# A message stage of a graph network: groups of four tiles, thin products padded to 128 rows, and a wait ahead of each pair of gathers

## What is computed

```
yv = edge_sh[:, 1:4]
m_s_tp = einsum('emi,ei->em', vs, yv) / sqrt(3)
w = silu(radial @ W_r1 * 8**-0.5) @ W_r2 * 8**-0.5
w_ss, w_vs, w_vt, w_st = split(w, 4, axis=1)
m_s = concat([ss * w_ss, m_s_tp * w_st])
m_v = concat([vs * w_vs, (ss x yv) * w_vt])
S, V = segment_sum(m_s, receivers), segment_sum(m_v, receivers)
```

## Time and profile before

| | us |
|---|---|
| median of 3 runs | 18873.3 |
| lowest, highest | 18834.3, 18887.8 |
| profiled execution | 18882.2 |
| its span | 18880.5 |

### The profile page before, as it was taken

The page is one execution under the profiler, slowest core; times in us unless marked ns, Lnnn a source line. Parts: engine busy times, 40 slices in busy tenths (PEclk is TensorE's granted clock), DMA queues, the critical chain, the costliest instruction groups (busy, mean ns, idle before and its releaser), DMA issues. The chain is left out here.

```text
span 18880.5 us, 358760 instructions
## 1 busy us (share of the span) xinstructions
PE 12828.6 (68%) x67608; PEld 9891.8 (52%) x67609; DVE 10946.8 (58%) x52171; ACT 4449.2 (24%) x12149; POOL 10487.9 (56%) x15826
## 2 busy tenths in 40 slices
PE   4457666666555556874888888759999998533333
PEld 2246666665333334763777777536666666422223
DVE  7778888886333334874565655426777775333333
ACT  7742222222111111441333333221111111200001
POOL 8878888887555554221555555205555552366664
PEclk9998999997555555996999999875555555655555
DMA  3001111111221112761555555401111112111113
GB/s 139 0 14 29 32 30 32 30 32 36 58 57 57 57 56 80 217 184 62 156 155 154 155 154 154 93 11 39 39 39 39 39 39 28 48 43 43 42 43 48
DMA packets 1925627, 1302.37 MB, mean 69 GB/s; under 512 B 1295244, under 2 KB 1680251, under 8 KB 1925564
## 3 DMA queue, kind: packets, MB, share of 16 engines
q1 hardware_dynamic: 1601276, 599.63, 14.0%
q0 software_dynamic: 324288, 701.98, 13.7%
HBM read 933.67 MB, written 373.78 MB: 69 GB/s over the span
## 5 line engine op out<-in xcount | busy, mean ns | idle before, releaser
L951 POOL DMA_INDIRECT edge_sv<-tab,edge_ix x1664 | 1569.0, 943 | 2169.5 <-DVE edge_ix L1332 1745.0
L951 POOL DMA_INDIRECT edge_fs<-tab_a,edge_ix x1664 | 1572.8, 945 | 1631.1 <-DVE edge_ix L1044 1176.4
L1759 POOL DMA_INDIRECT edge_ys<-tab,edge_ix x1664 | 1577.5, 948 | 1353.1 <-ACT edge_dl L1750 788.9
L610 POOL DMA_INDIRECT by_src<-send_row,send_pl x1664 | 1615.2, 971 | 1257.7 <-issue 1089.6
L662 PE MATMUL send_psX<-x_res,send_ohT 128*128 x3328 | 1315.1, 499 | 1188.9 <-ACT send_ohT L643 1077.5
L1803 PE MATMUL edge_psA<-edge_ys,edge_oh 128*128 128x128 f32 x3328 | 861.3, 441 | 1713.9 <-DVE edge_oh L1783 664.4
L460 POOL DMA_INDIRECT records<-place_pl,place_place x1568 | 1615.7, 1030 | 530.3 <-issue 492.1
L977 DVE TENSOR_TENSOR agg<-agg,edge_psA 128x256 f32 x3328 | 1379.7, 415 | 718.3 <-issue 358.0
L662 PEld LDWEIGHTS send_psX<-x_res,send_ohT 128*128 128x128 f32 x3328 | 833.5, 311 | 1758.9 <-issue 1758.9
L1803 PEld LDWEIGHTS edge_psA<-edge_ys,edge_oh 128*128 128x128 f32 x3328 | 740.9, 328 | 1834.4 <-DVE agg L1792 1355.5
L1398 PE MATMUL edge_psA<-edge_oh,edge_m 128*128 128x128 f32 x6656 | 1593.3, 421 | 0.6 <-DVE edge_m L1367 0.6
(11 more groups left out here) (319 smaller groups left out, 31986.0 us busy)
## 6 DMA issues: line engine op xcount, KB each, us to landing
edge_fd<-tab_b SPq DMA_DIRECT2D x1664, 128.0 KB
max_row<-by_src SPq DMA_DIRECT2D x392, 258.0 KB
running<-max_back POOLq DMA_DIRECT2D x392, 256.0 KB
records<-count_tmpl SPq DMA_DIRECT2D x64, 858.0 KB
send_pl<-records SPq DMA_DIRECT2D x832, 66.0 KB
edge_pl<-records SPq DMA_DIRECT2D x832, 50.0 KB
place_pl<-in_edge_attr SPq DMA_DIRECT2D x781, 50.0 KB
by_src<-send_row,send_pl POOLq DMA_INDIRECT x1664
```

Of the source, the lines that this page charges most:

```text
L610: pool.indirect_dma_start(S.by_src[:], bass.IndirectOffsetOnAxis(ap=at, axis=0), row[b][:, k, :], None, bounds_check=bound, oob_is_err=Fal ...
L951: pool.indirect_dma_start(rows[b % len(rows)][:, k, :], None, table[:], bass.IndirectOffsetOnAxis(ap=ix[b][:, k:k + 1], axis=0)).then_inc( ...
L1759: pool.indirect_dma_start(ys[b][:, k, :], None, table, bass.IndirectOffsetOnAxis(ap=ix[b][:, k:k + 1], axis=0)).then_inc(s_got[b], 16)
```

## The change

- Groups of four tiles (416 of them). Each group has one load, one transpose, one radial product, one weights product over 512 columns, and VectorE's message operations work on four tiles at once. `psA` takes two banks a group; `psT` and `psR` have one bank each instead of two.
- The radial and the weights product go over all 128 rows of their operands. The rows beyond 48 and 32 are zero; GpSimd clears them at the start.
- The one-hot moves from VectorE to ScalarE: four times Abs(dl - iota), then Relu(1 - gap) over 512 columns. ScalarE also copies indices and receiver rows (`ix`, `dl`). `sv`, `ix` and `dl` have four buffers, so the copy waits for the messages and the one-hot of the group four before.
- Block numbers are read four at once. The adds, and the message operations, stand in turns in VectorE's order.
- GpSimd waits, ahead of each pair of gathers, until the pair before the last one has landed (`paced`).

Lines that only rename G2 to G, and lines taken away whose counterpart is shown, are left out.

```diff
+def paced(pool, s_got, s_turn, b, r, depth, back):
+    o, n = before(b, r, back, depth)
+    if not isinstance(n, int) or n > 0:
+        pool.wait_ge(s_got[o], n * 32)
+        pool.sem_inc(s_turn, 1)
 def edge2_phase(nc, S, a, agg):
     with Phase(nc, "edge2") as ph:
-        M = 32
-        DEEP = 8
+        M, G, DEEP, NSV = 32, 4, 8, 4
...
+        ix = ph.sbs("ix", NSV, [P, G], I32)
+        dl = ph.sbs("dl", NSV, [P, G])
+        sv = ph.sbs("sv", NSV, [P, G, D])
...
+        oh = ph.sbs("oh", 2, [P, G, P])
         rT = ph.sbs("rT", 2, [P, P])
         hr = ph.sbs("hr", 2, [P, P])
-        vy = ph.sbs("vy", 2, [P, G2, 3, M])
...
-        psT = [ph.bank(f"psT{k}") for k in range(2)]
-        psR = [ph.bank(f"psR{k}") for k in range(2)]
...
+        m = ph.sbs("m", 2, [P, G, 2 * D])
+        wr1 = ph.sb("wr1", [P, G * 8])
+        wr2 = ph.sb("wr2", [P, G, D])
+        psT, psR = ph.bank("psT"), ph.bank("psR")
         psW = [ph.bank(f"psW{k}") for k in range(2)]
...
+        psA = [[ph.bank(f"psA{k}{h}") for h in range(2)] for k in range(2)]
...
+        s_got = [ph.sems(n, DEEP) for n in ("s_got_a", "s_got_b")]
...
         @block.sync
         def _(sp):
...
+            for k in range(G):
...
             def step(s, g, b, r):
                 wait(sp, s_m[b], r)
...
+                sp.dma_start(at[b][:], rec[:, bass.ds(g * G, G), R0:R0 + RN]).then_inc(s_rec[b], 16)
             runs(GT, [0], DEEP, sp, step)
         @block.gpsimd
         def _(pool):
...
-                 lambda s, g, b, r: gather_on(pool, b, ix, sv, S.tab_2, s_ix, s_got, s_turn, r))
+            for t in (wr1, wr2, *rT, *hr):
+                pool.memset(t[:], 0.0).then_inc(s_pad, 1)
+            pool.memset(one[:], 1.0).then_inc(s_pad, 1)
+            def step(s, g, b, r):
+                pool.wait_ge(s_ix[b], r + 1)
+                pool.sem_inc(s_turn, 1)
+                for k in range(G):
+                    if k % 2 == 0:
+                        paced(pool, s_got[k // 2], s_turn, b, r, DEEP, 1)
+                    pool.indirect_dma_start(sv[b % NSV][:, k, :], None, S.tab_2[:],
+                                            bass.IndirectOffsetOnAxis(ap=ix[b % NSV][:, k:k + 1], axis=0)
+                                            ).then_inc(s_got[k // 2][b], 16)
+            runs(GT, [0], DEEP, pool, step)
+        @block.scalar
+        def _(act):
+            act.wait_ge(s_pad, 7)
+            def step(s, g, b, r):
+                if s == 0:
+                    o, n = before(b, r, NSV, DEEP)
+                    wait(act, s_m[o], n)
+                    wait(act, s_oh[o], n)
+                    act.activation(ix[b % NSV][:], S.e_src[:, bass.ds(g * G, G)], ACT.Copy)
+                    act.activation(dl[b % NSV][:], S.e_dl[:, bass.ds(g * G, G)], ACT.Copy).then_inc(s_ix[b], 1)
+                elif s == 1:
+                    act.wait_ge(s_R[b], r + 1)
+                    o, n = two_before(b, r, DEEP)
+                    wait(act, s_W[o], n)
+                    act.activation(hr[b % 2][0:8 * G, :], psR[0:8 * G, 0:P], ACT.Silu, scale=8 ** -0.5).then_inc(s_hr[b], 1)
+                elif s == 2:
+                    act.wait_ge(s_T[b], r + 1)
+                    o, n = two_before(b, r, DEEP)
+                    wait(act, s_R[o], n)
+                    act.activation(rT[b % 2][0:G * RN, :], psT[0:G * RN, 0:P], ACT.Copy).then_inc(s_TT[b], 1)
+                else:
+                    act.wait_ge(s_ix[b], r + 1)
+                    o, n = before(b, r, 1, DEEP)
+                    wait(act, s_oh[o], n)
+                    for k in range(G):
+                        act.activation(gap[:, k, :], S.iota[:], ACT.Abs, scale=-1.0, bias=dl[b % NSV][:, k:k + 1]
+                                       ).then_inc(s_gap, 1)
+                    o, n = two_before(b, r, DEEP)
+                    wait(act, s_C[o], n)
+                    act.wait_ge(s_gap, g * G + G)
+                    act.activation(oh[b % 2][:], gap[:], ACT.Relu, scale=-1.0, bias=one[:]).then_inc(s_oh[b], 1)
+            runs(GT, [0, 1, 0, 2], DEEP, act, step)
         @block.vector
         def _(v):
...
+            v.memset(agg[:], 0.0).then_inc(s_add, 1)
...
+            def add(g, b, r, k):
+                half = psA[b % 2][k // 2]
+                rows = agg[:, bass.ds(blocks[k], 1), :].rearrange("p a c -> p (a c)")
+                if k == 0:
+                    v.wait_ge(s_C[b], r + 1)
+                v.wait_ge(s_add, g * G + k + 1)
+                v.tensor_tensor(rows, rows, half[:, (k % 2) * 2 * D:(k % 2 + 1) * 2 * D], ALU.add).then_inc(s_add, 1)
...
+            def step(s, g, b, r):
                 if s == 0:
...
+                    blocks[:] = nc.values_load_multi_w_load_instructions(
+                        S.blk[0:1, bass.ds(g * G, G)], engines=[mybir.EngineType.DVE], min_val=0, max_val=NBLK - 1)[1]
+                    return
+                if s in (2, 4, 6, 9):
+                    add(g, b, r, (2, 4, 6, 9).index(s))
+                    return
...
+                if s == 1:
+                    v.wait_ge(s_rec[b], (r + 1) * 16)
+                    v.wait_ge(s_got[0][b], (r + 1) * 32)
+                    v.wait_ge(s_got[1][b], (r + 1) * 32)
+                    o, n = two_before(b, r, DEEP)
+                    wait(v, s_C[o], n)
+                    v.tensor_tensor(vo[:, :, :, M:], vs, yv, ALU.mult).then_inc(s_op, 1)
+                elif s == 3:
+                    v.wait_ge(s_W[b], r + 1)
+                    v.tensor_tensor(su[b % 2][:], w[:, :, 2 * M:3 * M], ss, ALU.mult).then_inc(s_op, 1)
+                elif s == 5:
+                    v.wait_ge(s_op, g * OPS + 1)
+                    v.tensor_reduce(dot[b % 2][:], vo[:, :, :, M:].rearrange("p k i m -> p k m i"), axis=AX.X,
+                                    op=ALU.add).then_inc(s_op, 1)
                 elif s == 7:
...
-                    one_hot(v, oh[p][:], S, S.e_dl, g).then_inc(s_oh[b], 1)
...
+                    v.tensor_tensor(mo[:, :, 0:M], w[:, :, 0:M], ss, ALU.mult)
+                elif s == 8:
+                    v.tensor_tensor(vo[:, :, :, 0:M], thrice(w[:, :, M:2 * M]), vs, ALU.mult)
+                elif s == 10:
+                    v.wait_ge(s_op, g * OPS + 3)
+                    v.tensor_tensor(vo[:, :, :, M:], thrice(su[b % 2][:]), yv, ALU.mult).then_inc(s_op, 1)
                 else:
...
-            runs(GT, [0, 6, 4, 6, 4, 6, 4, 4], DEEP, v, lambda s, *x: step((0, 7, 1, 2, 3, 4, 5, 6)[s], *x))
...
-            runs(GT, [1, 2], DEEP, act, step)
+                    v.tensor_tensor(mo[:, :, M:2 * M], w[:, :, 3 * M:], dot[b % 2][:], ALU.mult).then_inc(s_m[b], 1)
+            runs(GT, [2, 0, 2, 0, 2, 0, 2, 0, 0, 2, 0, 0], DEEP, v, step)
         @block.tensor
         def _(pe):
...
+            pe.wait_ge(s_zero, 2)
+            pe.wait_ge(s_pad, 6)
             def step(s, g, b, r):
                 o, n = two_before(b, r, DEEP)
+                p, q = before(b, r, 1, DEEP)
                 if s == 0:
                     pe.wait_ge(s_m[b], r + 1)
                     pe.wait_ge(s_oh[b], r + 1)
...
+                    if not isinstance(g, int) or g >= 2:
+                        pe.wait_ge(s_add, (g - 2) * G + G + 1)
+                    for k in range(G):
...
+                            c = (k % 2) * 2 * D + q * D
+                            last = pe.matmul(psA[b % 2][k // 2][:, c:c + D], m[b % 2][:, k, q * D:(q + 1) * D],
                                              oh[b % 2][:, k, :], start=True, stop=True)
                     last.then_inc(s_C[b], 1)
                 elif s == 1:
                     pe.wait_ge(s_hr[b], r + 1)
                     wait(pe, s_m[o], n)
-                    pe.matmul(psW[b % 2][:, 0:G2 * D], hr[b % 2][0:8 * G2, :], wr2[0:8 * G2].rearrange("p k c -> p (k c)"),
+                    pe.matmul(psW[b % 2][:, :], hr[b % 2][:], wr2[:].rearrange("p k c -> p (k c)"),
                               start=True, stop=True).then_inc(s_W[b], 1)
                 elif s == 2:
                     pe.wait_ge(s_TT[b], r + 1)
...
-                    pe.matmul(psR[b % 2][0:8 * G2, 0:P], wr1[0:G2 * RN].rearrange("p k c -> p (k c)"), rT[b % 2][0:G2 * RN, :], start=True,
-                              stop=True).then_inc(s_R[b], 1)
+                    wait(pe, s_hr[p], q)
+                    pe.matmul(psR[0:8 * G, 0:P], wr1[:], rT[b % 2][:], start=True, stop=True).then_inc(s_R[b], 1)
                 else:
                     pe.wait_ge(s_rec[b], (r + 1) * 16)
...
-            runs(GT, [5, 3, 2, 1], DEEP, pe, step)
+                    wait(pe, s_TT[p], q)
+                    pe.sem_inc(s_go, 1)
+                    pe.transpose(psT[0:G * RN, 0:P], at[b][:].rearrange("p k c -> p (k c)"), S.ident[:]).then_inc(s_T[b], 1)
+            runs(GT, [4, 2, 1, 0], DEEP, pe, step)
```

More of the change, by code:

```diff
@@ L1274, in edge2_phase @@
-        sv = ph.sbs("sv", DEEP, [P, G2, D])
-        oh = ph.sbs("oh", 2, [P, G2, P])
+        at = ph.sbs("at", DEEP, [P, G, RN])
```

(38 more changed lines are left out.)

72 lines of the change are left out of this document (15 added, 57 removed).

## The result

The changed kernel takes **18,651.7 us** (median of 4 runs, 18,631.7 to 18,671.1) against 18,880.6 of the kernel before on the same chip (18,834.3 to 18,936.7): ratio 0.9887, interval 0.9857 to 0.9917. That is 229 us faster where I had forecast 780, and above the range, which ended at 18,550. The profiled execution took 18,651.4 us, its span is 18,649.8.

A forecast was written before the change was run, and what follows sets the result against it. GpSimd's gathers were to become the second message stage's bound: 416 groups x 5.54 us = 2,305 us in place of 3,083, 778 less; from 18,882 us that gives 18,104, about 18,100 us. Range 17,900 to 18,550, some 80%.

The forecast's parts named there:

- What bound the kernel, and the clock: Second message stage: TensorE bounds it at 1.2 GHz, 3.71 us a turn; padding the thin products raises the clock.
- The prices of PE, VectorE and ScalarE: Second message stage, per four-tile group: PE 6.47 us at the low clock, VectorE 4.4, ScalarE 3.3.
- The new wait at 0: GpSimd's wait ahead of each gather pair, second message stage: 1.1 us to spare, so costed at 0.
- GpSimd as the bound at 5.54 us a group: Second message stage: four gathers at 1.385 us pitch; 416 groups take 2,305 us in place of 3,083.
- the milder rival (c): Second message stage: standstills partly covered, 6.3 to 7.1 us a group, kernel 18,420 to 18,750 us; chance 8%.
- at most four gathers are now open at once: Argument against standstills in the second message stage: the cap on open gathers may be just what prevents them; no size.
- the likeliest case: Second message stage bound by GpSimd: kernel 17,880 to 18,200 us, with 18,100 as its time; chance 44%.
- one of transfers: Rival: transfers bound the second message stage at 6.12 us a group, 2,546 us, kernel 18,345 us; chance 20%.
- The severe (c): Second message stage: standstills of 2.07 us a group on top of 5.54, 7.61 in all, kernel 18,965 us; chance 12%.

The follow-up runs named there:

- e9: The kernel before with only its two thin products of the second message stage padded to 128 rows with zeros: 18,577.0 us, ratio 0.9816.
- e13: The kernel before with only its two thin products zero-padded to 128 rows, on another chip with standstills: 18,621.0 us, ratio 0.9852.
- e1: The changed kernel without the wait ahead of each pair of gathers, on a chip without standstills: 16,890.5 us, ratio 0.9462 to the kernel before.
- e10: The changed kernel gathering only the first four groups' sender rows, which later groups reuse, on a chip with standstills: 17,721.5 us, one execution.
- e8: The changed kernel without the wait ahead of each pair of gathers, on a chip with standstills: 18,487.3 us, ratio 0.9878 to the kernel before.
- e15: The changed kernel with a GpSimd clear of 128 f32 columns behind each gather and a wait for clears once a group: 18,648.9 us, ratio 0.9874.
- e18: The changed kernel with a GpSimd clear of 256 bf16 columns behind each gather and a wait for clears once a group: 18,493.8 us, ratio 0.9805.
- e12: The changed kernel with SP loading edge data of the first eight groups only, which later groups reuse: 18,678.3 us, one execution.
- e17: The changed kernel with two GpSimd clears of 128 bf16 columns behind each gather and a wait for clears once a group: 18,430.2 us, ratio 0.9777.

## Why the prediction was wrong

**What bound the kernel, and the clock: right in the main.** PE at 1.2 GHz was the bound. e9 and e13 show it: padding, with no other work changed, ended it. By the rule of the Trainium skill (TensorE: Matmul & The Clock Gate, Part 1) that the gate follows how busy PE has been, zero rows should have changed nothing; 0.50 at 100% busy and 0.97 at 66% contradict it. In the changed kernel the mean is 0.76, not near 1.0, because the clock falls in the standstills; where there are none it is 0.95 (e1) and 1.00 (e10).

**The prices of PE, VectorE and ScalarE: right.** I had 2.07 us for the weights product at the low clock; it takes 2.07, and 1.02 at the high one. VectorE: 4.4 us forecast, 4.36 in the trace of the changed kernel from the first product of one group to that of the next in dense stretches, 4.33 to 4.35 without gathers. ScalarE, groups by line:

```profile
L1361 ACT ACTIVATE edge_gap<-iota,edge_dl 128x128 f32<-128x128 f32 x1582 | 499.9, 387 | 0.0
L1366 ACT ACTIVATE edge_oh<-edge_gap,edge_one 128x512 f32<-128x512 f32 x396 | 286.1, 722 | 12.9
```

0.39 and 0.72 us, where I took 0.4 and 0.75.

**The new wait at 0: right here.** 20 us in 2,500, and no gain without it on a chip with standstills (e8). Its cost on a chip without them wasn't tried.

**GpSimd as the bound at 5.54 us a group: wrong on this chip.** This is the term that failed: the sum has PE, VectorE and ScalarE ready whenever GpSimd has gathered, and costs the standstills at 0. GpSimd does issue every 1.25 us, and on a chip without standstills the stage is even faster than I said (5.11). Here they add 2.3 us to VectorE's 4.36, and small waits the rest to 6.96. That is the milder rival (c), which I held at 8%, with its mechanism as written: they come where GpSimd issues without pause, as the last message stage had shown already. I let "at most four gathers are now open at once" speak against it, a guess with no row behind it, and put the likeliest case's 44% on a stage that issues like the last stage without behaving like it. The price that stood in the rows, 654 gathers in 1,000 us, 6.12 a group, is that of the last stage with its standstills; I read it as one of transfers. Transfers were not it: e1 issues 793 in 1,000 us and moves 57 GB/s where the changed kernel moves 41. The severe (c) failed in its own way: it added the standstills to 5.54, but GpSimd goes on issuing in most of each, so they add to VectorE's 4.36.

**What the engines lack is PE's word; why it is late is not shown.** The prediction took ScalarE's waits in the last message stage for something other than PE, since the products "had long ended" and the view named a DMA. By the semaphore updates of that trace, the copy that ran at 16,278.94 had waited for the product with the modelled end 16,265.95, whose semaphore was updated at 16,278.82, and the one at 16,300.66 for that with 16,270.83, updated at 16,300.52. It is thus the same event in both stages. Whether PE finishes late or its update travels late, and what gathers have to do with it, stays open. It hangs on the gather stream (e10), on its pitch (e15 to e18) and on the chip (e1), not on the pair waits (e8) nor on SP's loads (e12). The rule of the Trainium skill that DMA engines alternate between queues packet by packet (DMA: Bandwidth & Descriptors, Queues, rings and completion order) is neither borne out nor contradicted by this, against what the prediction said: what the halted engines waited for was no queue's.

## What to carry to other kernels

Before counting on an engine that is to run without pauses, look for a stage of the same kernel where it already does, and take all of that stage's rate and its shared idle times, not its best stretch. Try a change's parts alone: here two zero-padded products gave what the rewrite gave. When several engines stand together behind a busy issuer of gathers, slow the issuer a little and measure again. When a view names a releaser that can't be right, or none, see which semaphore was updated last and which instruction sets it: here that was PE, whose products the timeline shows as long done.

## What was not expected of the hardware

- On some chips, while GpSimd issues gathers 1.25 us apart, PE's semaphore updates come up to 12.6 us after the modelled ends of its products (over 3 us in 107 of 310 recorded for the radial product; some updates are missing from the trace), and ScalarE and VectorE halt together; with a mean of 1.6 us between gathers VectorE did not halt. On one chip of those used here it never came, at 1.25 us either; that chip runs the kernel before in 17,853 us where the others take 18,705 to 18,935. A result on one chip may not hold for the next: the same change without its waits gave 0.946 there and 0.988 elsewhere (e8).
- Zero rows raise TensorE's granted clock: 0.50 to 0.97, with the same useful work.
- In e17 a gather's issue took 1.1 to 1.3 us in place of 0.95 in 601 of 1,565 cases, and in all of these it overlapped one of VectorE's two products that read both operands from SBUF (L1419 and L1433, 384 columns); of the 808 that overlapped neither, 409 ran beside other work of VectorE and not one was long. So the pitch was not the sum of its idle parts.
